# A selective scan on one core: ScalarE's jobs in another order, the tap products of x packed, and the product of x and D on ScalarE

## The reference, cut

```
x = x + attn(cond(x, ...), ...)                     # the scan phase
x = x + ffn(cond2(x, cond_1024, ...), ...)          # the second phase, not touched

cond: conv of x (two taps here), proj -> B_t = softplus, C_t = tanh; u = x @ Ws
      state = decay * state + dt * b_t * u_t;  y0 = c_t * state;  out = y0 @ Wo + bo
attn: xn = layernorm(out);  xz = xn @ W_in;  x_br, z = split(xz)
      xb = silu(causal 4-tap convolution of x_br)
      Bm = xb @ W_b;  Cm = xb @ W_c;  delta = softplus(xb @ W_delta + b_delta)
      h = exp(delta * A) * h + delta * Bm * xb      # 1024 channels, 16 states, along time
      y = sum over states of h * Cm + xb * Dp
      out = (y * silu(z)) @ W_out + residual
```

## Time and profile before

| | us |
|---|---|
| median of 3 runs (lowest, highest) | 2659.27 (2657.55, 2660.13) |
| the profiled execution, its own time | 2653.91 |
| its span in the trace | 2651.9 |
| busy in the span: PE, DVE, ACT, POOL | 2309.5, 2265.5, 1669.0, 1728.4 |
| set-up and step -1, to the first scan | 102.8 |
| steps 1 to 14 (1767.0 / 14) | 126.2 each |

### The profile page before, as it was taken

How to read it: one execution, slowest core, us unless ns; L and a number is a source line. 1 busy time by engine, 2 the same in 40 slices (tenths; PEclk the granted TensorE clock), 3 DMA queues, 4 the chain that set the end, 5 groups by cost and what they waited for, 6 DMA issues and landing times. The chain is left out here.

```text
span 2651.9 us, 34212 instructions
## 1 busy us (share of the span) xinstructions
PE 2309.5 (87%) x11520; PEld 1586.2 (60%) x11520; DVE 2265.5 (85%) x2232; ACT 1669.0 (63%) x3332; POOL 1728.4 (65%) x2042
## 2 busy tenths in 40 slices
...
DMA packets 48299, 151.74 MB, mean 57 GB/s; under 512 B 8069, under 2 KB 8965, under 8 KB 45198
## 3 DMA queue, kind: packets, MB, share of 16 engines
...
...
## 5 line engine op out<-in xcount | busy, mean ns | idle before, releaser
L472 POOL TENSOR_TENSOR ring<-ring,Cbc 128x512 f32<-128x512 f32 x1024 | 1283.1, 1275 | 44.5 <-POOL carry L465 0.4
L864 DVE TENSOR_TENSOR_SCAN ring<-a_ps,ring 128x1024 f32<-128x1024 f32 x512 | 1168.0, 2281 | 106.7 <-ACT a_ps L702 105.2
L702 ACT ACTIVATE a_ps<-delta,nA 128x255 f32<-128x255 f32 x2048 | 852.9, 468 | 380.3 <-DVE ring L864 379.4
L1069 PE MATMUL yT_ps<-ident,ring 128*128 128x128 f32 x4096 | 588.1, 284 | 163.5 <-POOL ring L472 160.0
L1069 PEld LDWEIGHTS yT_ps<-ident,ring 128*128 128x128 f32 x4096 | 475.0, 145 | 282.2 <-POOL ring L472 241.9
L856 DVE TENSOR_TENSOR ring<-u_ps,Bbc 128x1024 f32<-128x1024 f32 x512 | 619.7, 1210 | 16.0 <-PE yT_ps L1069 9.3
L1035 PE MATMUL work<-xb,big 128*128 128x256 f32 x2048 | 476.8, 385 | 10.1 <-ACT zs L560 10.1
L1035 PEld LDWEIGHTS work<-xb,big 128*128 128x128 f32 x2048 | 385.5, 193 | 79.5 <-issue 16.9
L465 POOL TENSOR_TENSOR carry<-ring,half 128x4 f32<-128x4 f32 x512 | 127.1, 248 | 361.2 <-DVE ring L864 359.7
L1051 PE MATMUL work<-Wout,xb 128*128 128x512 f32 x512 | 237.7, 599 | 0.0
L1414 POOL TENSOR_TENSOR m<-m,pows 128x1 f32<-128x1 f32 x64 | 34.2, 549 | 311.4 <-DVE m L1546 311.4
...
## 6 DMA issues: line engine op xcount, KB each, us to landing
...
```

Of the source, the lines that this page charges most:

```text
L472: nc.gpsimd.tensor_tensor(hp, hp, Cbc[:, G * g + GP * c:G * g + GP * c + GP, :], ALU.mult)\
L702: r = nc.scalar.activation(a_ps[q % 2][:, i, 1:T], delta[:, par, dt, 1:T], ACT.Exp, scale=nA[:, dt, s:s + 1])
L864: dve.tensor_tensor_scan(ring[:, q % RING, :, :].rearrange("p g t -> p (g t)"), a_ps[q % 2][:, :, :].rearrange("p g t -> p (g t)"), ring[: ...
L1069: r = pe.matmul(yT_ps[:, tt, :], ring[:, q % RING, i, P * tt:P * tt + P], ident[:, :], is_transpose=True, start=False, stop=(g == NG - 1 a ...
```

## The change

ScalarE's plan changes. `prj` is at slot 4 and has only the Exp, `prj_ln` at slot 5 without a table load. A new job `visit` at slot 5 loads the table set of Silu, makes the Tanh, the two Silu of z for the block in the scan (before at slot 30 of the step ahead), and loads the set of Ln and Exp again. `silu` is cut in two halves, at slots 15 and 17, each with its two table loads. `zcopy(2)` and `dexp(1)` go from slot 27 to 26, `dln(0)` from 28 to 27. `keep_y0` goes from VectorE to ScalarE. The product of x and D goes from GpSimd to ScalarE (`skip`), at slots 3, 7, ... 27 for the next tile and at 29 for the first tile of the next block. VectorE's `gates0` goes from slot 4 to 3.

The four taps of x each had a matmul with 66 rows in use. Now the 64 state rows of taps 0 and 1 lie over each other in `yp` (one matmul), and the two further rows of those taps go to partitions 96 and 97 of `y0s`, under taps 2 and 3: three matmuls in place of four. `y0back` gets three more copies. The set-up of the weights follows (three transposes of 128 rows for each tile in place of four of 66, six small VectorE operations in place of four, one memset; not shown here). In step 0, `zsilu` moves from slot 3 to `visit`.

```diff
-        Mx = big[0][:, 0:4 * DI].rearrange("p (k c) -> p k c", k=4)
+        Mx = big[0][:, 0:3 * DI].rearrange("p (k c) -> p k c", k=3)
+        yp = big[0][:, 3 * DI:3 * DI + T]
...
@@ GpSimd
-                    if g == 0:
-
-                        wait(pool, s_xb, 2 * k + (2 if dt >= ND // 2 else 1))
-                        wait(pool, s_tr, NQ * k + NG * (dt - 2) + 1)
-                        nc.gpsimd.tensor_tensor(xdp[:, dt % 2, :], xb[:, par, dt, :],
-                                                V[:, V_DP + dt:V_DP + dt + 1].to_broadcast([P, T]), ALU.mult)\
-                            .then_inc(s_xdp, 1)
...
@@ ScalarE
+                    wait(act, s_c0, 6 * n)
                     nc.scalar.activation(e0[:, :], ps[0:N0, 0:T], ACT.Exp, bias=sc0[0:N0, 4:5]).then_inc(s_e0, 1)
 
-                    wait(act, s_c0, 6 * n)
-                    nc.scalar.activation(c0[:, :], ps[N0:P, 0:T], ACT.Tanh, bias=sc0[N0:P, 4:5]).then_inc(s_tanh, 1)
-
                 def prj_ln():
-                    nc.scalar.preload_act_table_set("natural_log_exp_and_others")
                     act.wait_ge(s_c0, 6 * n + 1)
                     nc.scalar.activation(e0[:, :], e0[:, :], ACT.Ln, bias=1.0).then_inc(s_l0, 1)
+
+                def visit():
+
+                    nc.scalar.preload_act_table_set("silu_and_others")
+                    if front:
+                        nc.scalar.activation(c0[:, :], work[BANK["PRJ"]][N0:P, 0:T], ACT.Tanh, bias=sc0[N0:P, 4:5])\
+                            .then_inc(s_tanh, 1)
+                    if scan:
+                        zsilu(k, par)
+                    nc.scalar.preload_act_table_set("natural_log_exp_and_others")
+
+                def keep_y0():
+
+                    if back:
+                        act.wait_ge(full[BANK["WOUT1"]], jobs_before("WOUT1", k) + 1)
+                    act.wait_ge(s_c0, 6 * n + 5)
+                    nc.scalar.activation(y0k[:, fp, :], y0[:, :], ACT.Copy).then_inc(s_c0, 1)
...
                     nc.scalar.activation(y0s[0:NY, fp, 0:3], y0s[0:NY, fp, T:T + 3], ACT.Copy).then_inc(s_yh, 1)
-                    act.wait_ge(s_yh, n + 1)
-                    nc.scalar.activation(y0s[0:NY, fp, 3:T + 3], ps[0:NY, 0:T], ACT.Copy).then_inc(free[BANK["YB"]], 1)
+                    act.wait_ge(s_yh, 2 * n + 1)
+                    nc.scalar.activation(y0s[0:NY, fp, 3:T + 3], ps[0:NY, 0:T], ACT.Copy).then_inc(s_yh, 1)
+                    act.wait_ge(s_yh, 2 * n + 2)
+
+                    nc.scalar.activation(yp[0:N0, :], y0s[0:N0, fp, 0:T], ACT.Copy)
+                    nc.scalar.activation(yp[N0:2 * N0, :], y0s[0:N0, fp, 1:T + 1], ACT.Copy)
+                    nc.scalar.activation(y0s[CROW:CROW + 2, fp, 2:T + 3], y0s[N0:NY, fp, 0:T + 1], ACT.Copy)\
+                        .then_inc(free[BANK["YB"]], 1)
...
-                def silu():
-                    for j in (ND // 2 - 2, ND // 2 - 1):
+                def silu(i):
+                    for j in (2 * i, 2 * i + 1):
                         act.wait_ge(free[BANK[f"XB{j}"]], jobs_before(f"XB{j}", k) + 1)
-                    for i in range(2):
-                        v = xb[:, fp, 4 * i:4 * i + 4, :].rearrange("p a b -> p (a b)")
-                        nc.scalar.activation(v, v, ACT.Silu).then_inc(s_xb, 1)
+                    v = xb[:, fp, 4 * i:4 * i + 4, :].rearrange("p a b -> p (a b)")
+                    nc.scalar.activation(v, v, ACT.Silu).then_inc(s_xb, 1)
                     nc.scalar.preload_act_table_set("natural_log_exp_and_others")
...
+                def skip(b, bp, dt):
+
+                    wait(act, s_xb, 2 * b + (2 if dt >= ND // 2 else 1))
+                    wait(act, s_tr, NQ * b + NG * (dt - 2) + 1)
+                    nc.scalar.activation(xdp[:, dt % 2, :], xb[:, bp, dt, :], ACT.Copy, scale=V[:, V_DP + dt:V_DP + dt + 1])\
+                        .then_inc(s_xdp, 1)
...
-                next_plan = {5: [prj], 6: [prj_ln], 8: [lambda: stats(0)], 9: [lambda: stats(1)], 10: [y0scale],
-                             11: [y0back], 14: [lambda: xcopy(0)], 15: [lambda: xcopy(1)], 16: [lambda: xcopy(2)],
-                             17: [lambda: xcopy(3), silu], 20: [bc], 21: [lambda: zcopy(0)], 23: [lambda: zcopy(1)],
-                             25: [lambda: dexp(0, False)], 27: [lambda: zcopy(2), lambda: dexp(1, False), lambda: dtail(0, False)],
-                             28: [lambda: zcopy(3), lambda: dln(0, False)], 30: [lambda: zsilu(n, fp)],
+                next_plan = {4: [prj], 5: [prj_ln], 8: [lambda: stats(0)], 9: [lambda: stats(1)], 10: [y0scale],
+                             11: [y0back], 13: [keep_y0], 14: [lambda: xcopy(0)], 15: [lambda: xcopy(1), lambda: silu(0)],
+                             16: [lambda: xcopy(2)], 17: [lambda: xcopy(3), lambda: silu(1)], 20: [bc],
+                             21: [lambda: zcopy(0)], 23: [lambda: zcopy(1)], 25: [lambda: dexp(0, False)],
+                             26: [lambda: zcopy(2), lambda: dexp(1, False)],
+                             27: [lambda: dtail(0, False), lambda: dln(0, False)], 28: [lambda: zcopy(3)],
                              31: [lambda: dexp(2, False)]}
...
+                    if q == 5 and (front or scan):
+                        visit()
                     if scan and q in turned:
                         gT(turned[q], par)
+                    if scan and g == 3 and dt < ND - 1:
+                        skip(k, par, dt + 1)
+                    if front and q == NQ - 3:
+                        skip(n, fp, 0)
...
@@ VectorE
-                next_plan = {4: [gates0], 5: [scan0], 13: [keep_y0]}
+                next_plan = {3: [gates0], 5: [scan0]}
...
@@ TensorE
-                    for tap in range(4):
-                        r = pe.matmul(ps[:, T * m:T * m + T], Mx[:, tap, c:c + P], y0s[:, fp, tap:tap + T],
-                                      start=(tap == 0), stop=(tap == 3))
+                    for i, rows in enumerate((yp[:, :], y0s[:, fp, 2:T + 2], y0s[:, fp, 3:T + 3])):
+                        r = pe.matmul(ps[:, T * m:T * m + T], Mx[:, i, c:c + P], rows, start=(i == 0), stop=(i == 2))
```

More of the change, by code:

```diff
@@ L33 @@
 NY = N0 + 2
+CROW = 96
 EPS = 1e-5
@@ L194, in scan_phase @@
         s_mxs = sem("s_mxs")
+        s_mtz = sem("s_mtz")
         s_mxp = sem("s_mxp")
@@ L644, in rowcopy @@
                     nc.scalar.activation(xw[:, c % 2, :], work[0][0:2, :], ACT.Copy).then_inc(s_rowcp, 1)
-                next_plan = {5: [prj], 6: [prj_ln], 8: [lambda: stats(0)], 9: [lambda: stats(1)], 10: [y0scale],
-                             11: [y0back], 14: [lambda: xcopy(0)], 15: [lambda: xcopy(1)], 16: [lambda: xcopy(2)],
-                             17: [lambda: xcopy(3), silu], 20: [bc], 21: [lambda: zcopy(0)], 23: [lambda: zcopy(1)],
-                             25: [lambda: dexp(0, False)], 27: [lambda: zcopy(2), lambda: dexp(1, False), lambda: dtail(0, False)],
-                             28: [lambda: zcopy(3), lambda: dln(0, False)], 30: [lambda: zsilu(n, fp)],
+                next_plan = {4: [prj], 5: [prj_ln], 8: [lambda: stats(0)], 9: [lambda: stats(1)], 10: [y0scale],
[4 more added lines that the diff above has]
+                             27: [lambda: dtail(0, False), lambda: dln(0, False)], 28: [lambda: zcopy(3)],
                              31: [lambda: dexp(2, False)]}
                 if isinstance(k, int) and k == -1:
-                    next_plan.update({27: [lambda: dexp(1, False), lambda: dtail(0, False)],
-                                      28: [lambda: dln(0, False), lambda: zcopy(2), lambda: zcopy(3)], 30: [], 31: []})
+                    next_plan.update({26: [lambda: dexp(1, False)], 28: [lambda: zcopy(2), lambda: zcopy(3)], 31: []})
                 scan_plan = {2: [lambda: dexp(3, True), lambda: dtail(1, True)], 6: [lambda: dln(1, True)]}
@@ L659, in step @@
                     scan_plan[1] = [lambda: dexp(2, True)]
-                    scan_plan[3] = [lambda: zsilu(k, par)]
                 turned = {13: 0, 20: 1, 28: 2}
@@ L772, in scan0 @@
                     dve.memset(mark[:, :], 0.0).then_inc(free[BANK["PRJ"]], 1)
-                def keep_y0():
-                    if back:
-                        dve.wait_ge(full[BANK["WOUT1"]], jobs_before("WOUT1", k) + 1)
-                    dve.wait_ge(s_c0, 6 * n + 5)
-                    dve.tensor_copy(y0k[:, fp, :], y0[:, :]).then_inc(s_c0, 1)
                 def mx_scale():
+                    dve.wait_ge(s_mtz, 1)
                     for m in range(ND):
@@ L785, in mx_scale @@
                         ps = abank[m // 4][:, NY * (m % 4):NY * (m % 4) + NY]
-                        for tap in range(4):
-                            r = dve.tensor_scalar(MTk[:, m, tap, :], ps, V[:, V_CW + 4 * m + tap:V_CW + 4 * m + tap + 1],
-                                                  None, ALU.mult)
+                        cw = [V[:, V_CW + 4 * m + tap:V_CW + 4 * m + tap + 1] for tap in range(4)]
```

(8 more changed lines are left out.)

11 lines of the change are left out of this document (6 added, 5 removed).

## The result

The changed kernel takes 2701.97 us (median of 4 runs, 2699.11 to 2703.71) against 2659.42 (4 runs): a ratio of 1.016, with a 95% interval of 1.0142 to 1.0178. The forecast had the sign and most of the places, but not the size: it said 13.8 us more, and it is 42.5. The time lies outside the range. The profiled execution took 2702.0 us with a span of 2700.1, so that in the frame of the two profiles the kernel lost 48.1 us.

The account below looks back on a forecast made before the run. VectorE was taken to set the pace, so its idle time counted. Fourteen full steps of +1.5 us (+20.6), with -5.7, -2.4, +0.6 and +0.7, gave +13.8 us: 2673.1 us, range 2646 to 2692.

Parts of the forecast that it names:

- Slots 3 to 11: Visit delays gT(3) and TensorE's output product by 2.2 us; TensorE takes up some, so scan 11 starts 0.9 us later.
- The 0.4 ahead of turn_y0: TensorE idle time of some 0.4 us ahead of turn_y0, said to take up part of the output product's 2.2 us delay.
- Slots 11 to 17: One stall of 3.60 us becomes two, 0.6 and 1.5, with packed taps and keep_y0 off VectorE: -1.9 us a step.
- Slots 25 to 31: zcopy(2), waiting for TensorE, now precedes a(26): scan 26 is 3.57 us late, scan 31 2.5 us late a step.
- The u_ps product: VectorE's slot 0 product was said to miss the gap between GpSimd's halves again, by 0.18 us: change 0.
- rival 2: u_ps falls into GpSimd's gap if 0.18 us earlier: 15 x -1.06 = -16 us, 2657 us; chance 0.18.
- Step -1: Set-up before the loop: fewer multiplies for x, half of Silu done earlier, no Tanh load ahead of Ln: -5.7 us.
- Step 0: zsilu leaves slot 3, where scan 3 waited 2.68 us, for -2.4 us; the rest of the step +0.6 us.
- Slots 11 to 17 of step 0: The full step's gain at these slots, -1.9 us, was said to hold in step 0 too.
- Step 15: gT(3) comes some 0.7 us later and TensorE is behind from there: +0.7 us.
- Rival 4: TensorE takes up none of the delay in slots 4 to 9: 14 x 1.3 = +18 us, 2691 us; chance 0.14.
- Rival 5: A drain at each table load makes gT(3) and slot 15 each 2.8 us later: 2740 us; chance 0.02.

Follow-up runs that it names:

- e2: The changed kernel with gT(3) at slot 5, ahead of visit, instead of slot 6: 2652.23 us.
- e1: The changed kernel with zcopy(2), dexp(1) and dtail(0) back at slot 27 and dln(0) at 28: 2653.9 us.
- e11: The kernel before with the visit alone, gT(3) still at slot 6: 2679.06 us.
- e3: The changed kernel with the edits of e1 and e2 together: 2619.02 us.
- e4: The changed kernel with unused transposes on TensorE, 15 ahead of the last transpose of turn_states(3) and 30 ahead of dl(2,0): 2687.24 us.
- e7: e3 with the packing of the taps undone, four matmuls a tile: 2633.62 us.
- e10: The kernel before with only zcopy(2) and dexp(1) moved to slot 26 and dln(0) to slot 27: 2683.64 us.
- e6: e3 with the product of x and D back on GpSimd: 2608.47 us.
- e8: e3 with visit undone: Tanh at slot 4, the SiLUs of z at slot 30 with their table loads, Exp still at slot 4: 2624.1 us.
- e9: e5 with the product of x and D on GpSimd: 2604.29 us.
- e5: e3 with dexp(2) moved to slot 0 of the next step and the last tile's product of x and D to slot 26: 2604.23 us.

## Why the prediction was wrong in size

**Slots 3 to 11 (+0.9; measured +2.37).** The order of events was right: gT(3) late behind the visit, TensorE's output product with it, scan 5 not waiting. The step that failed is "It now starts at 1014.9: 2.2 us late [...] so it comes out 0.9 late". It moves the six matmuls at the durations of the earlier trace rows. In after they take 2.04 and 2.80 us, against 1.58 for two in the earlier trace rows and 1.88 for four at full clock: 1.4 us, which with 0.9 makes 2.3. Measured from the start of scan 4 (1010.23 before, 1027.02 after), the output product starts 2.22 late, as said, and turn_y0 (1026.60 before, 1045.77 after) 2.38: 1.33 are added by the slower matmuls, and 1.17 are taken up at and right behind the 0.91 us of idle time at 1021.61. The 0.4 ahead of turn_y0, which the forecast took off too, isn't taken up: 0.41 still stands there, with ScalarE's stats as late as TensorE. e2 removes the loss whole, e1 none of it. The steps of e11 and e3 show that the lower clock costs 1.0 to 1.1 us there; e4 can't, as its first filler delays what it should only keep warm.

The row was also one of the faster ones. From the first's start to the last's end the six matmuls take 3.2 to 3.5 us in steps 5 to 14 of before (4.6 in after), but 4.3 to 4.4 in steps 1 to 4, more of them at the lower clock, and 4-11 is 28.94 in both. Before had the time to take that up; after, 2.2 us late, had not.

**Slots 11 to 17 (-1.9; measured -1.83).** Right in each part: stalls of 0.54 and 1.42 for the 0.6 and 1.5 said. e7 measures the packing at 0.87 of it.

**Slots 25 to 31 (+2.5; measured +4.04).** Scan 26 starts 6.89 us after scan 25 against 3.32 before: late by 3.57, to the hundredth what was said. From there the forecast had scan 31 18.04 us later, and it is 19.59. The step that failed is "The four parts that took 7.07 us from 1106.53 start at 1109.4", 9.5 us after scan 26. They start 11.05 after it, for dl(2, 0) and the two turnings ahead of them take 6.50 us (1121.74 to 1128.24). In e4, at full clock, they start 9.72 after scan 26. There and in eleven steps of e10, 25-31 is 24.74 to 25.16, where the forecast is 24.9. The mechanism was right and the term too small by the clock.

**The u_ps product (0; measured -1.01).** It takes 0.67 us, as rival 2 had it, but not by the 0.18 us that I named: scan 31 waits 0.8 longer than said (2.40 for 1.6), and GpSimd's last half has ended by then (the halves of scan 30, 1136.09 to 1138.59; u_ps starts at 1138.99). GpSimd's timeline of after the earlier trace rows:

```profile
1136.09 2.50 POOL L467 TENSOR_TENSOR ring<-ring,Cbc 128x512 f32<-128x512 f32 x2
1139.15 0.56 POOL L460 TENSOR_TENSOR carry<-ring,half 128x4 f32<-128x4 f32 x1 [0.56 <-DVE ring L887]
```

This agrees with the Trainium skill ("SBUF — State Buffer", SBUF: two separate sides), by which a VectorE operation with two SBUF inputs and a GpSimd operation that reads SBUF keep each other off the shared ports for a whole instruction: in e1, e3 and e4, where scan 31 waits 1.5 to 1.7 us, the product takes 1.5. The last row shows it from the other side: GpSimd's carry takes 0.56 us beside the product and ends at 1139.71, 0.05 behind it, where its median is 0.20.

**The ends.** Step -1 was said to be 5.7 shorter and is 5.75 (first scan at 97.08); e1 to e6, e8 and e9, with the same taps, have it between 95.5 and 99.5, and e7 without the packing has 98.37, so that the hit is partly luck. Of its terms, x's multiplies are shown: they run from 50.84 to 61.45, 10.6 us for 14.06. Step 0 was said to be 1.8 shorter and is 1.2 longer: 25-31 costs 3.75 there, and slots 0 to 4 give only 1.1, because gates0's first operation, now at slot 3, waits 0.54 for the Exp and takes 1.29 us, where it takes 0.26 without a wait in a full step. Those 1.57 go off the 2.68 of the earlier trace rows. VectorE's timeline of after in step 0, with the same operation in a full step under it:

```profile
115.95 1.29 DVE L777 TENSOR_SCALAR e<-e 64x256 f32<-64x256 f32 x1 [0.54 <-ACT e L496]
...
1022.19 0.26 DVE L777 TENSOR_SCALAR e<-e 64x256 f32<-64x256 f32 x1
```

Slots 11 to 17 of step 0 give 0.15 us where 1.9 was said. Scan 15 waits 2.17 us there and not 0.54: the matmuls of x that xcopy(1) waits for take 1.06, 1.91, 0.99 and 1.03 us from 154.98, the first two at the lower clock, where the next take 0.60 and 1.03 (159.23, 159.66).

Step 15 was said to be 0.7 longer and is 4.2: slots 4 to 11 take 33.08 us for 28.85. VectorE waits there for the turned states. The output product is late and slow here too (2.04 and 5.84 us from 2068.60, for 1.60 and 4.46 before), and then 16 turnings take 3.61 us, where before (the last fence) had 1.94. TensorE was idle ahead of neither; what it ran just before were 32 matmuls of two columns (3.63 us), with no wait in either kernel. VectorE's timeline of after, then TensorE's of after and of before:

```profile
2088.75 1.22 DVE L879 TENSOR_TENSOR ring<-u_ps,Bbc 128x1024 f32<-128x1024 f32 x1 [3.26 <-PE yT_ps L1091]
```

```profile
2083.31 3.63 PE L1121 MATMUL work<-Wtap,delta 128*128 128x2 f32 x32
2086.80 3.61 PE L1091 MATMUL yT_ps<-ident,ring 128*128 128x128 f32 x16
```

```profile
2036.12 3.63 PE L1099 MATMUL work<-Wtap,delta 128*128 128x2 f32 x32
2039.61 1.94 PE L1069 MATMUL yT_ps<-ident,ring 128*128 128x128 f32 x16
```

In e2 and e3 it is 29.02 and 29.12, but in e5 to e9, with gT(3) at the same place, it is 31.8 to 33.2, and in e10, where no job of this step differs from before, 32.59, with the turnings at 3.65. So the place of gT(3) doesn't decide it alone; what does stays open, and it is 3 to 4 us of each of these kernels.

**The sum.** 14 steps of +3.5 are 49.0; with -5.75, +1.2 and +4.2 that is 48.6, and the spans differ by 48.2. The median moved only 42.5, since the profiled execution of before lay 5.4 under its median and that of after on it. Of the 34 us that the forecast missed in the frame of the profiles (48.1 - 13.8), 28 lie in the 14 full steps (1.5 us for each of the two places, less 1.0 for the u_ps product), 3 in step 0 and 3.5 in step 15.

**The rivals.** Rival 4 (TensorE takes up nothing, 2691) came nearest for 4-11, but for another reason: TensorE did take up 1.17 us of the 1.3, and lost 1.33 by the clock. Rival 5 (a drain at each table load) didn't happen. ScalarE's timeline of after the earlier trace rows has the instruction behind each load 0.01 or 0.02 us after its end; the Trainium skill's 1.38 us of drain ("ScalarE: Activation LUTs", What ACT_TABLE_LOAD costs) isn't seen:

```profile
1023.98 0.40 ACT L500 ACTIVATE e<-e 64x256 f32<-64x256 f32 x1
1024.39 1.28 ACT L504 ACT_TABLE_LOAD   x1
1025.69 0.47 ACT L506 ACTIVATE c<-work,sc 64x256 f32<-64x256 f32 x1
1026.19 2.00 ACT L599 ACTIVATE zs<-zs 128x1024 f32<-128x1024 f32 x2
1028.21 1.28 ACT L510 ACT_TABLE_LOAD   x1
1029.50 1.66 ACT L728 ACTIVATE a_ps<-delta,nA 128x255 f32<-128x255 f32 x4
```
